# Two mixture-of-experts stages of a graph network: weights prepared in earlier stages, and results added tile by tile in DRAM

## What is computed

```
# layer 0 (input: layernorm(x)), 8 experts, hidden width 192, the best 2 of 8 by softmax
top_w, top_i = top_k(softmax(x @ router_w.T), 2); top_w = top_w / top_w.sum()
for e in range(8):
    w_e = sum(top_w * (top_i == e))
    out = out + w_e * (gelu(x @ w1[e] + b1[e]) @ w2[e] + b2[e])
# layer 1 (input: layernorm(x)), the same sizes, a router with added biases
W1 = w_fast1 + m_gate1 * w_slow1 + h_fast1      # per expert
h  = square(relu(x @ W1 + b1))
W2 = w_fast2 + m_gate2 * w_slow2 + h_fast2      # per expert
out = out + gate[:, e] * (h @ W2 + b2)
```

## Time and profile before

| what | value |
|---|---|
| median of 3 runs | 1617.39 us |
| the profiled execution | 1618.41 us, span 1616.6 us, mean granted clock 0.847 |
| TensorE matmul busy | 76% |
| VectorE busy | 56% |
| ScalarE busy | 46% |
| GpSimd busy | 42% |

### The profile page before, as it was taken

One profiled execution on the slowest core, in us unless ns is written; L12 is line 12 of the kernel. 1 busy time (PEld: TensorE's weight loads), 2 busy tenths in 40 slices (PEclk: granted clock), 3 DMA queues, 4 the chain that ended last, 5 costly groups with the idle time before them and its releaser, 6 DMA issues. The chain is left out here.

```text
span 1616.6 us, 32695 instructions
## 1 busy us (share of the span) xinstructions
PE 1232.5 (76%) x9846; PEld 928.5 (57%) x9847; DVE 910.4 (56%) x1717; ACT 737.3 (46%) x1097; POOL 673.7 (42%) x820
## 2 busy tenths in 40 slices
PE   8997665975684179638899999999999768631992
PEld 6775555974544067427566666666666455431781
DVE  8953676876554520173666666566665367676002
ACT  8994303753113265341555554555554341222661
POOL 0086836774566213112455555555555400010330
PEclk9999775886785589859999999999999869755996
DMA  1001200002004344476789999899998866467336
GB/s 57 1 1 20 63 16 1 1 1 78 11 3 147 106 140 138 144 249 240 232 253 270 287 283 272 255 275 277 282 288 244 231 185 190 112 164 175 119 128 182
DMA packets 112001, 247.49 MB, mean 153 GB/s; under 512 B 23590, under 2 KB 48675, under 8 KB 111798
## 3 DMA queue, kind: packets, MB, share of 16 engines
q1 hardware_dynamic: 78422, 157.29, 30.2%
q0 software_dynamic: 33504, 89.21, 21.8%
HBM read 216.18 MB, written 53.64 MB: 167 GB/s over the span
## 5 line engine op out<-in xcount | busy, mean ns | idle before, releaser
L644 PE MATMUL r_pO<-ring,r_rowsT 128*128 x2520 | 422.9, 327 | 0.0
L644 PEld LDWEIGHTS r_pO<-ring,r_rowsT 128*128 128x128 f16 x2520 | 244.4, 98 | 155.2 <-issue 2.0
L1843 DVE SCALAR_TENSOR_TENSOR ring<-q_wstage,ring 128x768 f16<-128x768 f32 x198 | 175.1, 954 | 55.9 <-ACT ring L1802 54.6
L1783 POOL DMA_INDIRECT acc_dram<-r_msg,r_scol x70 | 128.9, 1842 | 159.3 <-PE r_pT L1904 104.5
L1802 ACT ACTIVATE ring<-q_wstage 128x768 f16<-128x768 f32 x198 | 148.8, 829 | 25.8 <-issue 25.8
L1831 ACT ACTIVATE r_msg<-r_pO,slot_inv 128x768 f32<-128x768 f32 x70 | 62.9, 898 | 193.2 <-PE r_pO L644 192.9
L477 POOL DMA_INDIRECT inv_col<-qinv_dram,pair_col x112 | 116.2, 1037 | 77.1 <-POOL pair_col L490 69.9
L427 POOL DMA_INDIRECT slot_dram<-table_record,table_rowi x80 | 101.9, 1274 | 102.7 <-DVE table_rowi L297 76.2
L390 PE MATMUL acc<-oh_d,oh_s 125*125 125x512 f16 (+1 forms) x800 | 134.9, 308 | 0.0
L1548 PE MATMUL f_ps<-f_down,f_hT 97*128 (+1 forms) x408 | 76.0, 338 | 48.7 <-DVE f_hT L1394 43.3
L1241 POOL DMA_INDIRECT y_dram<-f_parts,f_row x34 | 33.6, 988 | 179.5 <-ACT f_parts L1446 179.5
(11 more groups left out here) (400 smaller groups left out, 2502.6 us busy)
## 6 DMA issues: line engine op xcount, KB each, us to landing
q_wstage<-in_L_gnn_W_rel_dram SPq DMA_DIRECT2D x33, 2304.0 KB, 14.2
f_stage<-in_L_ffn_w_dram SPq DMA_DIRECT2D x16, 576.0 KB, 7.1
f_stage<-y_dram SPq DMA_DIRECT2D x10, 672.0 KB
stage<-in_L_gnn_W_dram SPq DMA_DIRECT2D x6, 768.0 KB, 5.9
q_wstage<-in_L_ffn_w_fast_dram SPq DMA_DIRECT2D x6, 768.0 KB, 5.3
q_wstage<-in_L_ffn_w_slow_dram SPq DMA_DIRECT2D x6, 768.0 KB, 7.3
q_wstage<-in_L_ffn_h_fast_dram SPq DMA_DIRECT2D x6, 768.0 KB, 9.0
f_stage<-in_L_ffn_w_fast_dram SPq DMA_DIRECT2D x8, 576.0 KB, 5.7
```

Of the source, the lines that this page charges most:

```text
L644: ins = eng.matmul(out, x, w[:, h * n:(h + 1) * n], start=first and x is xh and w is wh, stop=last and x is xl, **kw)
L1783: eng.indirect_dma_start(out=K.acc_dram[u % 2], out_offset=bass.IndirectOffsetOnAxis(ap=scol[:, u:u + 1], axis=0), in_=msg[:, u, :], in_of ...
L1843: ins_ = eng.scalar_tensor_tensor(wring[:, slot, 1, k, :], wstage[:, slot, k, :], W_SCALE, wring[:, slot, 0, k, :], ALU.mult, ALU.subtract)
```

## The change

- The up weights of layer 0 are loaded and cut in the attention "a2": SP loads (`load_up`), ScalarE cuts the high halves at its end of the block (`cut_up_hi`), VectorE the low halves of two experts behind each of the first four tiles of `residual`. `ffn_phase` has no `cut_up` any more.
- Layer 0 cuts four down weights ahead of the logits (`EARLY_CUTS`) and four behind the table. The down stage has five buffers (three before). ScalarE cuts 5, 6 and 7 behind the exponential and ahead of `evict(0)`.
- The down weights of layer 1 are merged and cut on VectorE in the tile loop of layer 0, half an expert a tile, flat on 128 partitions (128x1152). The halves go to a new DRAM tensor `down_dram`. Layer 1 loads them with four DMAs at its start and has no merges or cuts.
- x is stored ("seeded") into an accumulator in DRAM behind the store of xn: `y_dram` in layer 0 (625 rows now), the output itself in layer 1. Each scatter adds to it, drops empty places by a bounds check, and waits for the scatter before it. Layer 0 then loads x back tile by tile and measures it; layer 1 ends with its last scatter.
- `load_small` (now four loads) moves from the attention to the end of SP's list in "q1"; the gates `mg2` are loaded in the tile loop of layer 0.
- Some scratch tensors of the edge and attention stages share memory, and the table has three columns for four.

```diff
             eng.dma_start(B["bias"][:, :], finish["bias"].partition_broadcast(P)).then_inc(s["bias_loaded"], 16)
             eng.wait_ge(s["bias_loaded"], 16)
             if heads == 1:
-                load_small(K, eng, s["small_loaded"])
-                eng.wait_ge(s["small_loaded"], 16 * 5)
+                finish["sync"](eng)
...
         gat_attend(K, "a1", B, HEADS, HD, h1, {"bias": ins["L0_gnn_b1"], "vector": elu_vector, "scalar": elu_scalar})
         gat_project(K, "g2", B, B["g"], None, ins["L0_gnn_W2"], ins["L0_gnn_a_src2"], ins["L0_gnn_a_dst2"], 1, C, h2)
+        UPS = 4
+        up_stage = B["wparts"][:, :, :, :].rearrange("p a k n -> p (a k n)").bitcast(FP32).rearrange("p (u k f) -> p u k f", u=UPS, k=KC)
+        up_loaded = [K.sem("up_chunk%d" % u) for u in range(UPS)]
+        up_hi, up_lo = K.sem("up_hi"), K.sem("up_lo")
+        def load_up(eng):
+            for e in range(EXP):
+                if e >= UPS:
+                    eng.wait_ge(up_lo, e - UPS + 1)
+                eng.dma_start(up_stage[:, e % UPS, :, :], ins["L0_ffn_w1"][e].rearrange("(k p) f -> p k f", p=128)).then_inc(up_loaded[e % UPS], 16)
+        def cut_up_hi(eng, s):
+            for e in range(EXP):
+                eng.wait_ge(up_loaded[e % UPS], 16 * (e // UPS + 1))
+                eng.activation(K.up[:, 0, :, e, :], up_stage[:, e % UPS, :, :], ACT.Copy, scale=W_SCALE).then_inc(up_hi, 1)
+        def cut_up_lo(eng, e):
+            eng.wait_ge(up_hi, e + 1)
+            eng.scalar_tensor_tensor(K.up[:, 1, :, e, :], up_stage[:, e % UPS, :, :], W_SCALE, K.up[:, 0, :, e, :], ALU.mult, ALU.subtract
+                                     ).then_inc(up_lo, 1)
...
-        gat_attend(K, "a2", B, 1, C, h2, {"bias": ins["L0_gnn_b2"], "vector": residual, "scalar": lambda eng, s: None})
+                for e in range(2 * i, min(2 * i + 2, EXP)):
+                    cut_up_lo(eng, e)
+        gat_attend(K, "a2", B, 1, C, h2, {"bias": ins["L0_gnn_b2"], "sync": load_up, "vector": residual, "scalar": cut_up_hi})
...
+                eng.dma_start(down_stage[:, e % DOWNS, :].rearrange("p (t c) -> p t c", t=2),
+                              ins[L + "w2"][e].rearrange("(t p) c -> p t c", p=FH)).then_inc(s_down[e % DOWNS], 16)
+            def load_set(e):
+                for a, name in enumerate(("w_fast2", "w_slow2", "h_fast2")):
+                    eng.dma_start(sets[:, e % 2, a, :], ins["L1_ffn_" + name][e].rearrange("f c -> (f c)").rearrange("(p n) -> p n", p=128)
+                                  ).then_inc(s_set[e % 2], 16)
...
+                for e in range(DOWNS):
+                    load_down(e)
                 with nc.allow_non_contiguous_dma("a bias to a column per hidden tile"):
                     eng.dma_start(b1[:, :, :], ins[L + "b1"].rearrange("e (t p) -> p e t", p=FH)).then_inc(s["small_loaded"], 16)
+            else:
+                for a in range(2):
+                    for t in range(2):
+                        eng.dma_start(w_down[0:FH, a, :, t, :], K.down_dram[:, a, :].rearrange("e (t p c) -> t p e c", t=2, c=C)[t]).then_inc(s["down_loaded"], 16)
             eng.wait_ge(T.s["lo_ready"], NT)
             eng.dma_start(K.xn_dram.rearrange("(i p) c -> p i c", p=P), parts[:, :, :, :].rearrange("p i a c -> p i (a c)")).then_inc(s["stored"], 16)
...
-                for e in range(UPS, EXP):
-                    eng.wait_ge(s["w_lo"], e - UPS + 1)
-                    load_up(e)
+            eng.dma_start(acc.rearrange("(i p) c -> p i c", p=P), K.x[:, :, :]).then_inc(s["seeded"], 16)
             eng.wait_ge(s["b2_ready"], 1)
             for e in range(EXP):
                 eng.dma_start(w_down[FH:FH + 1, :, e, 1, :], b2p[e:e + 1, :, :]).then_inc(s["b2_placed"], 16)
+            if layer == 0:
+                for e in range(DOWNS, EXP):
+                    eng.wait_ge(s["cut_lo"], e - DOWNS + 1)
+                    load_down(e)
+                eng.wait_ge(s["cut_lo"], EXP)
+                eng.dma_start(mg2[:, :], ins["L1_ffn_m_gate2"].partition_broadcast(128)).then_inc(s_set[0], 16)
+                load_set(0)
+                load_set(1)
+                for e in range(EXP):
+                    eng.wait_ge(s["set_cut"], e + 1)
+                    eng.dma_start(K.down_dram[e].rearrange("a (p n) -> p a n", p=128), halves).then_inc(s["set_stored"], 16)
+                    if e + 2 < EXP:
+                        load_set(e + 2)
+                eng.wait_ge(s["set_stored"], 16 * EXP)
             eng.wait_ge(s["b2_placed"], 16 * EXP)
...
-            both = K.y_dram[0:2 * N, :].rearrange("(a n) c -> n a c", a=2)
-            for i in range(NT):
...
-                    eng.dma_start(sums[p:q, i, :, :], both[i * P + p:i * P + q, :, :]).then_inc(sums_loaded[i], 16)
-            if layer == 1:
+            eng.wait_ge(s["scattered"], 16 * FTILES)
+            if layer == 0:
                 for i in range(NT):
-                    eng.wait_ge(s["added"], i + 1)
                     for p, q in ((0, 112), (112, P)):
-                        eng.dma_start(K.out[i * P + p:i * P + q, :], K.x[p:q, i, :]).then_inc(s["out_stored"], 16)
-                eng.wait_ge(s["out_stored"], 32 * NT)
+                        eng.dma_start(K.x[p:q, i, :], acc[i * P + p:i * P + q, :]).then_inc(summed[i], 16)
...
-                eng.indirect_dma_start(out=K.y_dram, out_offset=bass.IndirectOffsetOnAxis(ap=row[:, t:t + 1], axis=0),
-                                       in_=y[:, t % YS, :], in_offset=None).then_inc(scattered[t % YS], 16)
+                if t == 0:
+                    eng.wait_ge(s["seeded"], 16)
+                else:
+                    eng.wait_ge(s["scattered"], 16 * t)
+                eng.indirect_dma_start(out=acc, out_offset=bass.IndirectOffsetOnAxis(ap=row[:, t:t + 1], axis=0),
+                                       in_=y[:, t % YS, :], in_offset=None, bounds_check=N - 1, oob_is_err=False, compute_op=ALU.add
+                                       ).then_inc(s["scattered"], 16)
             if layer == 0:
...
                 link(eng.tensor_scalar(en[:, :, 0:2], en[:, :, 0:2], 0.1, None, ALU.mult))
-                merge(0), merge(1)
-                cut_down(0), cut_down(1)
             else:
-                for e in range(EXP):
-                    cut_up(e)
...
+            link(eng.tensor_scalar(empty[:, :], table[:, 0, :], 0.0, 2.0 * N, ALU.is_equal, ALU.mult))
+            eng.scalar_tensor_tensor(row[:, :], table[:, 0, :], -1.0, empty[:, :], ALU.add, ALU.add).then_inc(s["rows_ready"], 1)
...
-            for e in range(2 * layer, EXP):
-                if layer == 1:
-                    merge(e)
-                cut_down(e)
+            if layer == 0:
+                for e in range(EARLY_CUTS, EXP):
+                    cut_down(e)
+            def merge(e, part):
+                w, slow, third = (sets[:, e % 2, a, :] for a in range(3))
+                if part == 0:
+                    eng.wait_ge(s_set[e % 2], 48 * (e // 2 + 1) + (16 if e % 2 == 0 else 0))
+                    link(eng.scalar_tensor_tensor(w, slow, mg2[:, e:e + 1], w, ALU.mult, ALU.add))
+                    eng.tensor_tensor(w, w, third, ALU.add).then_inc(s["set_merged"], 1)
+                else:
+                    eng.wait_ge(s["set_merged"], e + 1)
+                    if e:
+                        eng.wait_ge(s["set_stored"], 16 * e)
+                    link(eng.tensor_scalar(halves[:, 0, :], w, W_SCALE, None, ALU.mult))
+                    eng.scalar_tensor_tensor(halves[:, 1, :], w, W_SCALE, halves[:, 0, :], ALU.mult, ALU.subtract).then_inc(s["set_cut"], 1)
             for t in range(FTILES):
                 eng.wait_ge(s["h_hi"], t + 1)
                 eng.tensor_tensor(hT[0:FH, t % 2, 1, :, :], h[:, t % 2, :, :], hT[0:FH, t % 2, 0, :, :], ALU.subtract).then_inc(s["h_lo"], 1)
-            for i in range(NT):
-                eng.wait_ge(sums_loaded[i], 32)
-                eng.tensor_tensor(K.x[:, i, :], K.x[:, i, :], sums[:, i, 0, :], ALU.add).then_inc(s["summed"], 1)
-                eng.wait_ge(s["summed"], i + 1)
-                eng.tensor_tensor(K.x[:, i, :], K.x[:, i, :], sums[:, i, 1, :], ALU.add).then_inc(s["added"], 1)
...
+                    merge(t // 2, t % 2)
+            if layer == 0:
+                for i in range(NT):
+                    eng.wait_ge(summed[i], 32)
                     measure(K, eng, i)
...
             if layer == 0:
-                for e in range(EXP):
-                    cut_up(e)
                 for e in range(DOWNS):
                     cut_down(e)
             else:
                 eng.wait_ge(s["norm_ready"], 1)
                 eng.activation(en[:, :, 2], en[:, :, 2], ACT.Sqrt).then_inc(s["root_ready"], 1)
-                cut_down(0), cut_down(1)
                 eng.wait_ge(s["norm_ready"], 2)
                 eng.activation(tok[:, :, 1], tok[:, :, 1], ACT.Sqrt).then_inc(s["root_ready"], 1)
             eng.wait_ge(s["diff_ready"], 1)
```

(23 more changed lines are left out.)

159 lines of the change are left out of this document (62 added, 97 removed).

## The result

The changed kernel takes 1595.17 us (median of 4 runs, 1593.12 to 1600.81), the kernel before in the same session 1617.97: ratio 0.9866, 95% interval [0.9834, 0.9898]. It is 1.3% faster, 23 us, a third of the 68 us forecast, and the time lies above the range of 1524 to 1580.

The account below looks back on a forecast made before the run. TensorE bounds the relation stage and first feed-forward tile loop; elsewhere it waits on fronts and returns through memory. 4 - 19 + 4 - 7 + 11 - 42 - 19 = -68 us: 1549 against the median; eight in ten: 1524 to 1580.

Parts of the forecast that it names:

- Mean 5.6, 0.4 over the period: First feed-forward loop: adding scatters take 4.8 us quiet, 6.5 beside set loads; a lag of 4 us at the loop's end.
- rival A: Chain of adding scatters becomes the bound, slower than before: about 1705 us in both loops; 1600 to 1625 4%, above 3%.
- A mild A in the first loop: Scatters at 7.0 us a tile in the first loop alone: +27, 1576 us; 1561 to 1582 had 22%, shared with C.
- The turning point of 7.2 us: Scatter time per tile at which the chain eats the 68 us gain over 34 tiles of both loops: 5.2 + 2.0.
- Hidden, if the sets are there: First feed-forward loop: VectorE's half-merges of second-stage down weights fit in each 5.2 us period; 0, bound +15 us.
- First front: First feed-forward, start to first down product: earlier table and gathers, last ScalarE cut near 554 us; -19 us.
- rival B: Seed and small loads cost nothing: -7 us in the first stage, -11 ahead of the relation stage, 1531 us; 20%.
- Ends: From last scatter: first feed-forward -7 us (-4 to -12), second feed-forward to the span's end -19 (-14 to -22).
- Rivals C and D: C: first loop starves on sets, attention loses 11 us: 1571, 22% with mild A. D: VectorE meets logits late: 2 us.
- attention: Second attention layer: weight cuts hold GpSimd's copies, +7 us; five small loads leave, -3; net +4, range -5 to +11.
- small loads: Ahead of the relation stage: four small loads on SP delay the loop's opening; +11 us, between 0 and 15.
- second front: Second feed-forward, start to first down product: merges, cuts and waits go; -42 us, range -36 to -46.

Follow-up runs that it names:

- e10: Changed kernel with plain scatters without waits in the first feed-forward stage and each scatter issued two tiles later in both stages: 1559.11 us, ratio 0.9662.
- e4: Changed kernel with the loads of six of the eight sets of second-stage down weights left out, merges and stores kept: 1581.21 us, ratio 0.9775.
- e6: Changed kernel with the accumulator's seed issued behind the bias copies and down loads, and split in 112 and 13 partitions: ratio 0.985.
- e2: Changed kernel with each tile's adding scatter to its own DRAM array, no wait between scatters, results never summed: 1568.59 us, ratio 0.9703.
- e3: Changed kernel with each tile's scatter to its own DRAM array, writing instead of adding, no wait, results never summed: 1554.08 us, ratio 0.9611.

## Why the prediction was wrong

The step that failed is this one: "Beside the set loads (roughly half the loop) perhaps 6.5. Mean 5.6, 0.4 over the period [...] Five y buffers keep TensorE from it at first." Its size and its path are both wrong, and the sign that the prediction had named for this, scatters more than 6 us apart, is there.

- **Size.** The first loop's scatters stood 7.45 us apart, not 5.6. An adding scatter landed in 6.1 us (median, up to 10.0), and the period is the landing and about half a us more: in the second stage, with no set loads beside it, a median landing of 5.5 us makes a period of 6.06. In the first stage many landings lie well above the median. I had scaled the 5.7 us of the earlier trace rows down to 4.8 for part-empty tiles; they landed hardly sooner. And I let the sets load through half of the loop; SyncE issues them until 661.9, some 87 of the loop's 119.5 us.
- **Path.** I had named the buffers that stand between TensorE and the chain, and not the queue. Gather t+5 is issued behind scatter t, so each wait for a landing is a wait of the gather. This needs no full y buffer. I wrote "with GpSimd's gathers in the same queue" under rival A and priced nothing for it.
- **Where I had it right in the rivals.** A mild A in the first loop, 7.0 us a tile, was priced at +27 and 1576; at 7.45 the same sum gives +34, and +31.0 (35.0 less the 4 forecast) was measured. (Its 1705 for both loops takes off 7 where the sum holds only 4 for them; 1708 is right.) The turning point of 7.2 us was for both loops; the second ran at 6.06, so the kernel stayed faster.
- **Sets.** "Hidden, if the sets are there": VectorE's merges are hidden (e10). But the sets slowed gathers from 4.4 to 7.7 us, a price that the prediction put on scatters alone. With late-issued gathers it costs up to 15 us (e4), with early ones, beside plain scatters, nothing (e10).
- **First front**, -13.4 for -19: the order of the waits was as forecast, but ScalarE's last cut ended 62 us into the stage instead of 56, since the eight bias copies, which my sum had left out, took 23.8 us to issue behind the seed. e6 gives 7.7 us back, about the 7 that rival B put on it.
- **Ends** of the two stages: -11.6 for -7, -22.2 for -19, 7.8 us better than forecast. The second loop's own chain (+10.9, forecast 0) takes more than that.
- **Rivals C and D** did not come: in the first loop VectorE waits for a set once, 2.40 us, and it takes the logits as soon as TensorE has them (1.74 us of waiting for TensorE at 530.38).
- **Right**: attention +4.8 (+4; whether its two terms, +7 and -3, are right one by one isn't shown), small loads +12.6 (+11), second front -40.3 (-42), table at 38.6 (38) and first down product at 63.6 (64) us into their stages.

On the seed, the Trainium skill (DMA: Bandwidth & Descriptors, "Why a DMA increments its semaphore by 16 and not by 1") made me put the seed's price in its shape of 125 rows. The delay did come (SyncE's 23.77 us behind the seed), and the trace agrees with the page: a DMA share of 0.33 while such stores go out, near 5 of 16 engines. But e6 changed place and shape at once, so how much of its 7.7 us is the shape's isn't shown. Could the wait between scatters simply go? The same page ("Rules for kernel authors") says that an accumulating DMA reads its destination and writes it later, so a write that lands in between is lost, and to wait for the earlier one's semaphore. No run here shows such a loss; I kept the wait wherever two adding scatters shared an array.

What stays open: how the adding costs 14.5 us without the waits (e2 and e3), whether ScalarE's late weights are all of the 4.6 to 5.7 us that the relation stage loses with the small loads inside it, and how much of e6 belongs to the seed's place and how much to its split.

## What to carry to other kernels

When a change adds a wait to one instruction, list what the same engine has to issue behind it, and read the lead time of those instructions, not of the waiting one: here a scatter's wait stalled gathers that had nothing to do with it. Where an instruction that fetches ahead stands behind one that puts results away, try the second one a few tiles later: here that cost three lines and, once nothing waited for landings, was worth 19 us of loop. And price a chain of adding scatters, each waiting for the one before, by its landing measured beside the transfers that will really run with it (here 5.5 to 6.1 us, for a period of 6.06 to 7.45), against the tile's period of 5.2: it saves an end, once, and costs its excess in every tile.

## What the runs showed of the hardware

- An adding indirect scatter of 128 x 768 f32 takes GpSimd 1.59 us to issue and lands in 5.7 us (median), a plain one 1.01 and 3.0 us, in otherwise equal kernels (e2, e3). Company counts as much: plain ones land in 3.0 us in the second stage of e3, in 4.5 in its first, and in 5.9 in e10's first loop.
- Indirect gathers of 128 x 1536 f16 land in 4.4 us (before, median), 5.2 beside adding scatters (second stage), and 7.7 and 6.7 in first loops that move 211 and 284 GB/s in all (changed kernel, e10): more bytes per us don't make them later by themselves.
- Stores of 125 rows (1.92 MB) keep the 16 DMA engines busy to 0.33 and move 130 GB/s (changed kernel, 520 to 545 us).
- GpSimd's one-column copies stretch while VectorE cuts weights, here one that otherwise takes 0.2 us to 7.57 us, which ends with four cuts of 6.75 us together (timeline, changed kernel):

```profile
521.12 7.57 POOL L491 COPY slot_inv<-inv_col 128x1 f32 x1
```
```profile
521.89 6.75 DVE L1296 SCALAR_TENSOR_TENSOR f_down<-f_stage,f_down 96x1536 f16<-96x1536 f32 x4
```
- With the same matmuls TensorE's busy time in the first loop is 83.85 us at a mean clock of 1.00 (e10) and 94.64 at 0.90 in the changed kernel, where it had idled before its transposes. 1.00 is 2.4 GHz. Not all of the difference is the clock: in the second loops of e3 and of the changed kernel, at 1.00 both, busy time is 83.5 and 91.9 us.
